# Image-wise adapter stack on one core: the second product with x2 as the stationary operand and W2 streamed in 512 columns

## The chip, the cores and the metric

The kernel runs on one core of a Trainium2 chip. The metric is device time in microseconds (us) of one execution. Before the change the median of three runs is 509.82 us (509.17 to 510.21).

The core's engines work side by side and meet at semaphores only: PE (TensorE, matmuls into the PSUM banks; its weight loads have a row of their own, PEld), DVE (VectorE), ACT (ScalarE), POOL (GpSimd), and SP (SyncE), which here issues every DMA.

## The reference

The inputs are 8 images x of 256 rows (tokens) by 1024, all float32. For each image, with `a` and `l` the two adapter numbers of that image:

```python
x0 = x + dequantise(x)                      # 8 thresholds, 8 deltas, 8 zero points
x1 = x0                                     # called x1 in the kernel
x2 = x1 + x1 @ W1[a].T                      # W1: 8 matrices 1024x1024
x3 = x2 + x2 @ W2.T + 0.5*(x2 @ A2[l]) @ B2.T     # W2 1024x1024, rank 32
out = x3 + (x3 @ B3[a].T) @ A3[a].T         # rank 16
```

`dequantise` takes for each element the group that its absolute value falls in, rounds x/delta, clips it to 64 levels and multiplies back; above the largest threshold it gives 0.

## The kernel before

**Layout.** The 1024 features are 8 tiles (k or o) of 128 partitions; the 256 tokens lie along the free dimension. An image is 8 x 256 columns on 128 partitions, worked in two chunks of 4 tiles (1024 columns).

**Quantiser.** Per image 16 steps, 8 groups for each chunk. ACT makes `tq` and `mask`, DVE makes the level (`value`, L499), clips it (`clamp`, L509) and lays it over `y` by the mask (`select`, L523). At a chunk's end `cut_y` (L529) and `add_y` (L534) write that chunk of x1. The quantiser runs one image ahead of the matmuls, so DVE and ACT carry the small jobs of image b in fixed slots between the steps of image b+1. The slots are tables of step numbers (`ACT_X2`, `DVE_X2`, `W2_AT` and others), one column for the first images and one for the later.

**W1 phase.** PE multiplies in full float32 (`w1b` stationary, x1 of 256 columns moving, L742) into four banks `x2_bank`, one for each pair of output tiles: first all output tiles with the first chunk of x1, then with the second. A float32 matmul leaves two records in the trace, so that the 64 matmuls of an image are 128 records.

**x2.** As a pair is done, DVE adds x1 (`finish_x2`, L588) into a tile x2, ACT rounds that to float32r (`x2h`, L381), and DVE takes the remainder (`x2l`, L595).

**Second product.** The identity was added to W2 once, and W2 was split into `w2h` and `w2l`, and so into three products per tile: w2h with x2h, w2l with x2h, w2h with x2l. Each is a float32r matmul with a 128x128 tile of W2 stationary and x2 of 256 columns moving (L709, 192 for an image). The low-rank part goes through `low_bank` (L715, 24 matmuls with `vh`, `vl`), is rounded into `lows`, and comes back with `uhh` and `ul0` (L726, L727: 2 matmuls for each of the 8 output tiles, 16 for an image). The tables behind v and u (A2 with G = B3 + B3 W2, and E = B2 + A3 (B3 B2) with A3) are chosen per image by DMA from DRAM and rounded and split again on ACT and DVE for each image (`round_v`, `split_v` L603, `round_u`, `split_u` L608).

**Start.** PE first makes the 8 tiles of G and the four blocks of E. W2 comes in slices of 512 KB into two places `stage`; for each slice POOL adds the identity (L317), ACT rounds (L407), POOL takes the remainder (L319).

**Order of the work.** Each engine executes its list in program order; SP's one queue likewise, so that a DMA stands behind every wait that SP passes before it.

Of the kernel before, what the change touches and what calls it, by code (L numbers as in the profile page):

```python
# [5 lines left out]
def quantised_residual_adapter_stack(nc, x, params, w1, w2t, w2n, b3t, b2n, b2r, a3, la, ids_b, ids_a,  # L6
                                     own_rows, low_scale, ident, out, e_dram, g_dram):

# [22 lines left out]
    ALU = mybir.AluOpType  # L31
# [7 lines left out]
    NL = la.shape[0]  # L39
# [9 lines left out]
    OUT_BANKS = 2  # L49
# [5 lines left out]
    TQ, MK = 4, 2  # L55

    ctx = ExitStack()
    with ctx:
# [12 lines left out]

        xin = sb("xin", [P, KT, T])
        x1 = sb("x1", [P, KT, T])
        x2 = sb("x2", [P, 2, 2 * T])
        x2h = sb("x2h", [P, KT, T], f32r)
        x2l = sb("x2l", [P, KT, T], f32r)
        outb = sb("outb", [P, PAIRS, 2 * T])
        w1b = sb("w1b", [P, OT, KT * P])
        w2h = sb("w2h", [P, OT, KT * P], f32r)
        w2l = sb("w2l", [P, OT, KT * P], f32r)  # L80
        stage = sb("stage", [P, 2, KT * P])
# [12 lines left out]
        scrap = sb("scrap", [P, 2])  # L94
        lscale = sb("lscale", [P, 1])
        ua = sb("ua", [P, D])
        uhh = sb("uhh", [P, D], f32r)
        ul0 = sb("ul0", [P, D], f32r)
        va = sb("va", [P, KT, R2])
        vg = sb("vg", [P, KT, R3])  # L100
        vh = sb("vh", [P, KT, P], f32r)
        vl = sb("vl", [P, KT, P], f32r)
        lowh = sb("lowh", [P, T], f32r)
        lows = sb("lows", [P, T], f32r)
        ycut = uq[:, 1, :]

        b3s = chunk(x1, 1).rearrange("p (k r) -> p k r", k=KT)
        a3s = outb[:, 0:2, :].rearrange("p j t -> p (j t)")
        b2s = outb[:, 2, 0:KT * R2].rearrange("p (k r) -> p k r", k=KT)
        dmask = outb[:, 2, KT * R2:KT * R2 + NA * R2].rearrange("p (a r) -> p a r", a=NA)  # L110
        eye = outb[:, 3, 0:P]
        rows = outb[:, 3, P:P + NA]
        gsb = ua[:, :].rearrange("p (a k r) -> p a k r", a=NA, k=KT)
        b2rep = x2[:, :, :].rearrange("p j t -> p (j t)")
        w2g = w1b
        e_place = [outb[:, 0, :], outb[:, 1, :], outb[:, 2, :], x2[:, 1, :]]


        x2_bank = [pb(f"x2_bank{i}") for i in range(PAIRS)]
        out_bank = [pb(f"out_bank{i}") for i in range(OUT_BANKS)]  # L120
        low_bank = pb("low_bank")
        de_bank = pb("de_bank")
        e_bank = [low_bank, de_bank] + out_bank

# [4 lines left out]
        b_in = sem("b_in")  # L129
        small_in = sem("small_in")  # L130
        w2g_in = [sem(f"w2g_in{j}") for j in range(KT // 2)]
        stage_in = [sem(f"stage_in{c}") for c in range(2)]
        u_in = sem("u_in")
        v_in = sem("v_in")

        store_done = [sem(f"store_done{c}") for c in range(2)]
        pads = sem("pads")
        ua_zero = sem("ua_zero")
# [9 lines left out]
        x1_ready = sem("x1_ready")  # L148
        pair_done = sem("pair_done")
        x2_ready = sem("x2_ready")  # L150
        out_ready = sem("out_ready")
        e_out = sem("e_out")
        diag_ready = sem("diag_ready")
        x2h_ready = sem("x2h_ready")
        x2l_ready = sem("x2l_ready")
        vh_ready = sem("vh_ready")
        vl_ready = sem("vl_ready")
        uh_ready = sem("uh_ready")
        ul_ready = sem("ul_ready")
# [4 lines left out]
        dmask_ready = sem("dmask_ready")  # L164
        g_tiles = sem("g_tiles")
        g_ready = sem("g_ready")
        e_done = sem("e_done")
        e_ready = sem("e_ready")
# [5 lines left out]
        def group_of(s):  # L174

            return G - 1 - s % G
# [5 lines left out]
        def x2_pairs(n):  # L182

            return PAIRS + n

        def out_pairs(n):

            return OUT_BANKS + n


        @block.sync
        def _(sp):
# [10 lines left out]
            def load_u(a):  # L203
                for r in (0, DUP):
                    sp.dma_start(ua[r:r + R2, :], e_dram[bass.ds(a, 1)].rearrange("a r n -> (a r) n")) \
                        .then_inc(u_in, 16)
                    sp.dma_start(ua[r + R2:r + R, :], a3[bass.ds(a * R3, R3), :]).then_inc(u_in, 16)

            def load_v(a, lab):
                sp.dma_start(va[:, :, :], la[bass.ds(lab, 1)].rearrange("a p k r -> (a p) k r")) \  # L210
                    .then_inc(v_in, 16)
                sp.dma_start(vg[:, :, :], g_dram[bass.ds(a, 1)].rearrange("a p k r -> (a p) k r")) \
                    .then_inc(v_in, 16)
# [24 lines left out]
            a0, lab0 = ids_of(0)  # L238


            def store_e(e, done):
                h, n = divmod(e, 2)
                sp.wait_ge(e_ready, e + 1)
                sp.dma_start(e_dram.rearrange("(h a) r n -> h (a r) n", h=EH)[h, :, n * 512:(n + 1) * 512],
                             e_place[e]).then_inc(done, 16)

            def load_w2(i):

                sp.dma_start(stage[:, i % 2, :], w2t[i, :, :]).then_inc(stage_in[i % 2], 16)

            load_w2(0)
            load_w2(1)
# [3 lines left out]
            sp.wait_ge(g_ready, 2)  # L256
            sp.dma_start(g_dram.rearrange("a p k r -> p a k r"), gsb[:, :, :, :]).then_inc(store_done[0], 16)
            sp.wait_ge(x1_ready, 1)
            load_x(1, 0)
            sp.wait_ge(store_done[0], 16)  # L260
            load_v(a0, lab0)
            E_AFTER = (3, 3, 4, 4)
            for i in range(2, OT):
                if i == OT // 2:
                    sp.wait_ge(x1_ready, 2)
                    load_x(1, 1)
                sp.wait_ge(w2l_ready, i - 1)
                load_w2(i)
                for e in range(2 * EH):
                    if i == E_AFTER[e]:  # L270
                        store_e(e, e_out if e < 2 * EH - 1 else store_done[1])
                if i == E_AFTER[-1] + 1:
                    sp.wait_ge(store_done[1], 16)
                    sp.wait_ge(e_out, 16 * (2 * EH - 1))
                    sp.wait_ge(ua_zero, 1)
                    load_u(a0)

            def next_batch(b, ahead):

                a, lab = ids_of(b + 1)  # L280
                for j in range(PAIRS):
                    sp.wait_ge(pair_done, 2 * PAIRS * b + j + 1)
# [4 lines left out]
                sp.wait_ge(vl_ready, 4 * (b + 1))  # L287
                sp.wait_ge(ul_ready, b + 1)
                load_v(a, lab)
                load_u(a)  # L290
                for c in range(2):
                    sp.wait_ge(out_ready, out_pairs(PAIRS * b + 2 * c + 2))
                    store(b, c)
                if ahead:
                    sp.wait_ge(x1_ready, 2 * (b + 1) + 2)
                    load_x(b + 2, 1)

# [3 lines left out]
            for j in range(PAIRS):  # L301
                sp.wait_ge(out_ready, out_pairs(PAIRS * LAST + j + 1))
                sp.dma_start(out[LAST, :, j, :], outb[:, j, :]).then_inc(store_done[j // 2], 16)
            for c in range(2):
                sp.wait_ge(store_done[c], 16 * (B + 2))
# [3 lines left out]
        def _(pool):  # L309
# [4 lines left out]
            for o in range(OT):  # L314
                pool.wait_ge(stage_in[o % 2], 16 * (o // 2 + 1))
                diag = stage[:, o % 2, o * P:(o + 1) * P]
                nc.gpsimd.tensor_tensor(diag, diag, eye, ALU.add).then_inc(diag_ready, 1)  # L317
                pool.wait_ge(w2h_ready, o + 1)
                nc.gpsimd.tensor_tensor(w2l[:, o, :], stage[:, o % 2, :], w2h[:, o, :].bitcast(f32),  # L319
                                        ALU.subtract).then_inc(w2l_ready, 1)  # L320
                if o == 1:
                    pool.wait_ge(store_done[0], 16)
                    nc.gpsimd.memset(ua[:, :], 0.0).then_inc(ua_zero, 1)

        D_AT, G_AT = 9, (10, 12)
        E_AT = (STEPS + 2, STEPS + 2, STEPS + 3, STEPS + 3)
        W2_AT = (11, 14, 16, 17, STEPS + 5, STEPS + 6, STEPS + 7, STEPS + 9)  # L330
# [3 lines left out]
        ACT_V, DVE_V = 2, 3  # L334
        ACT_U, DVE_U = (7, 4, 4, 4), (8, 5, 5, 5)
        ACT_X2 = ((4, 5, 6, 7), (6, 7, 8, 9), (7, 8, 9, 10), (8, 9, 10, 10))
# [7 lines left out]
        def _(act):  # L344
# [47 lines left out]
            def round_u(b, first):  # L392
                act.wait_ge(u_in, 64 * (b + 1))
                if not first:
                    act.wait_ge(pair_done, 2 * PAIRS * b)
# [443 lines left out]
```

## Time and profile before

| what | before |
|---|---|
| median of 3 runs | 509.82 us |
| span of the profiled execution | 508.2 us (the records hold no other time of that execution) |
| PE busy | 479.8 us, 94% |
| DVE busy | 437.5 us, 86% |
| ACT busy | 356.1 us, 70% |
| POOL busy | 36.8 us, 7% |
| DMA | 67.0 MB, 132 GB/s over the span |
| granted clock of PE, mean | 0.979 of full |

The span runs from the first to the last instruction of the profiled execution, 1.6 us less than the median of the runs. A busy share is the time in which the engine had at least one instruction under way. Matmuls overlap in the pipeline (a record of 0.28 us starts every 0.12 us), so the cost of one is read from the distance of the starts, never from its own length.

### The profile page before, as it was taken

The page shows a single profiled execution, that of the slowest core. Times are in us where ns is not written, and L with a number is a line of the kernel's source. Part 1 is how long each engine was busy: PE and PEld are TensorE (multiplying, and loading weights), DVE is VectorE, ACT ScalarE, POOL GpSimd, SP SyncE. Part 2 cuts the span into 40 slices and gives each one's busy share as a digit, 9 for nine tenths or more (in the row PEclk, how much of TensorE's full clock was granted, in tenths as well). Part 3 has the DMA queues.
Part 4 walks back from the last instruction along what each step waited for, and adds up shares of the span by engine and source line. Part 5 has one row for each costly group of instructions (what it writes and reads, how often), then busy time and mean ns, then how long its engine had stood idle before and what let it go on. Part 6 is the DMA issues. An engine that isn't in the chain of part 4 may idle for free.

```text
span 508.2 us, 8219 instructions
## 1 busy us (share of the span) xinstructions
PE 479.8 (94%) x3056; PEld 446.1 (88%) x3056; DVE 437.5 (86%) x521; ACT 356.1 (70%) x400; POOL 36.8 (7%) x24
## 2 busy tenths in 40 slices
PE   3979589799999999999999999999999999999997
PEld 3968278798899989998899989998899889998997
DVE  4999999999999999999999989998999979941300
ACT  6996767798878796798778866987498867710110
POOL 2123407600000000000000000000000000000000
PEclk9979879899999999999999999999999999999999
DMA  8965161660284027410661057402741246110011
GB/s 283 414 271 182 42 195 53 268 226 2 83 331 130 0 67 278 157 41 36 221 235 50 0 164 251 126 0 83 258 160 41 78 170 212 41 41 0 0 41 41
DMA packets 18112, 67.00 MB, mean 132 GB/s; under 512 B 2608, under 2 KB 5936, under 8 KB 14000
## 3 DMA queue, kind: packets, MB, share of 16 engines
q1 hardware_dynamic: 18096, 66.81, 37.8%
q8 instruction: 7, 0.11, 0.1%
q14 instruction: 9, 0.07, 0.0%
HBM read 56.84 MB, written 9.96 MB: 131 GB/s over the span
## 4 chain that ended last, share of the span: by engine, by line
PE 58%; DVE 28%; issue 6%; POOL 3%; ACT 2%; DMA 1%; DVEq 0%; SPq 0%; ACTq 0%
PE x_bank L742 28%; PE out_bank L709 25%; DVE y L523 11%; DVE uq L509 6%; DVE tq L499 4%; PE low_bank L715 3%; POOL w2l L319 2%; DVE uq L529 2%; DVE x L534 2%; DVE x2l L595 1%; DVE y L509 1%; PE out_bank L727 1%; PE out_bank L726 1%; ACT tq L352 1%; DMA xin<-x 1%
## 5 line engine op out<-in xcount | busy, mean ns | idle before, releaser
L742 PE MATMUL x_bank<-x,w1b 128*128 128x256 f32 x1024 | 227.8, 385 | 11.5 <-DVE x L534 11.5
L742 PEld LDWEIGHTS x_bank<-x,w1b 128*128 128x128 f32 x1024 | 197.6, 194 | 40.0 <-DVE x L534 12.6
L352 ACT ACTIVATE tq<-xin,magic,rdelta 128x1024 f32<-128x1024 f32 x128 | 157.4, 1232 | 3.5 <-DMA xin<-x 3.2
L368 ACT ACTIVATE mask<-absx,negtop 128x1024 bf16<-128x1024 f32 x112 | 128.2, 1144 | 36.4 <-DVE y L523 34.5
L523 DVE COPY_PREDICATED y<-mask,uq 128x1024 f32<-128x1024 int16 x112 | 150.5, 1344 | 0.1
L709 PE MATMUL out_bank<-x2h,w2h 128*128 128x256 f32 x512 | 145.5, 284 | 0.4 <-ACT outb L414 0.4
L709 PE MATMUL out_bank<-x2h,w2l 128*128 128x256 f32 x512 | 145.4, 284 | 0.0
L709 PE MATMUL out_bank<-x2l,w2h 128*128 128x256 f32 x512 | 145.2, 284 | 0.0
L499 DVE TENSOR_SCALAR tq<-tq,par 128x1024 f32<-128x1024 f32 x128 | 109.6, 856 | 5.8 <-ACT tq L352 3.9
L709 PEld LDWEIGHTS out_bank<-x2h,w2h 128*128 128x128 f32 x512 | 98.5, 192 | 0.6 <-ACT outb L414 0.6
L709 PEld LDWEIGHTS out_bank<-x2h,w2l 128*128 128x128 f32 x512 | 98.7, 193 | 0.0
L709 PEld LDWEIGHTS out_bank<-x2l,w2h 128*128 128x128 f32 x512 | 98.7, 193 | 0.0
L509 DVE TENSOR_SCALAR uq<-tq,ylow,yhigh 128x1024 f32<-128x1024 f32 x112 | 93.4, 834 | 1.1 <-issue 0.9
L381 ACT ACTIVATE x2h<-x 128x512 fp32r<-128x512 f32 x32 | 20.0, 625 | 54.0 <-DVE x L588 53.9
L588 DVE TENSOR_TENSOR x<-x_bank,x 128x512 f32<-128x512 f32 x32 | 21.9, 685 | 27.1 <-PE x_bank L742 27.0
L414 ACT ACTIVATE outb<-out_bank 128x512 f32<-128x512 f32 x32 | 18.6, 582 | 19.2 <-PE out_bank L727 19.2
L361 ACT ACTIVATE absx<-xin 128x1024 f32<-128x1024 f32 x16 | 16.9, 1054 | 19.1 <-DVE uq L529 19.1
L319 POOL TENSOR_TENSOR w2l<-stage,w2h 128x1024 fp32r<-128x1024 f32 x8 | 25.6, 3198 | 29.3 <-ACT w2h L407 29.3
L595 DVE TENSOR_TENSOR x2l<-x,x2h 128x512 fp32r<-128x512 f32 x32 | 22.0, 689 | 3.2 <-ACT x2h L381 2.8
L529 DVE SCALAR_TENSOR_TENSOR uq<-absx,top,y 128x1024 f32<-128x1024 f32 x16 | 20.6, 1285 | 0.4
L715 PE MATMUL low_bank<-x2h,vh 128*128 128x256 f32 x64 | 19.6, 307 | 1.3 <-DVE x2l L595 1.3
L726 PE MATMUL out_bank<-lows,uhh 128*128 128x256 f32 x64 | 17.0, 287 | 3.4 <-DVE lows L613 3.4
(64 smaller groups left out, 284.7 us busy)
## 6 DMA issues: line engine op xcount, KB each, us to landing
w1b<-w SPq DMA_DIRECT2D x32, 1024.0 KB, 4.9
xin<-x SPq DMA_DIRECT2D x16, 512.0 KB, 4.7
out<-outb SPq DMA_DIRECT2D x14, 512.0 KB, 2.8
w1b<-w2n SPq DMA_DIRECT2D x4, 1024.0 KB, 12.0
stage<-w2t SPq DMA_DIRECT2D x8, 512.0 KB, 5.3
ua<-e_dram SPq DMA_DIRECT2D x16, 128.0 KB, 3.6
va<-la SPq DMA_DIRECT2D x8, 128.0 KB, 3.7
ua<-a SPq DMA_DIRECT2D x16, 64.0 KB, 3.6
```

What stands on the lines that cost most here:

```text
L319: nc.gpsimd.tensor_tensor(w2l[:, o, :], stage[:, o % 2, :], w2h[:, o, :].bitcast(f32), ALU.subtract).then_inc(w2l_ready, 1)
L352: nc.scalar.activation(tq[:, s % TQ, :], chunk(xin, c), ACT.Identity, bias=magic[:, 0:1], scale=rdelta[:, g:g + 1]).then_inc(t_ready, 1)
L368: nc.scalar.activation(mask[:, s % MK, :], absx[:, :], ACT.Relu, bias=negtop[:, g:g + 1], scale=1.0).then_inc(mask_ready, 1)
L499: nc.vector.tensor_scalar(tq[:, s % TQ, :], tq[:, s % TQ, :], -MAGIC, par[:, 1, g:g + 1], ALU.add, ALU.mult).then_inc(u_ready, 1)
L509: nc.vector.tensor_scalar(clamped_y, tq[:, s % TQ, :], ylow[:, g:g + 1], yhigh[:, g:g + 1], ALU.max, ALU.min).then_inc(clamped, 1)
L523: nc.vector.copy_predicated(y[:, :], mask[:, s % MK, :].bitcast(i16), uq[:, s % 2, :]) \
L529: nc.vector.scalar_tensor_tensor(ycut, absx[:, :], top[:, G - 1:G], y[:, :], ALU.is_gt, ALU.mult).then_inc(y_cut, 1)
L595: nc.vector.tensor_tensor(x2l[:, pair, :].rearrange("p k t -> p (k t)"), x2[:, j % 2, :], x2h[:, pair, :].rearrange("p k t -> p (k t)").bi ...
L709: nc.tensor.matmul(into, w[:, o, cut], xs[:, k, :], start=(o % 2 == 0 and k == 0 and i == 0), stop=False, skip_group_check=True)
L715: last = nc.tensor.matmul(low_bank[:, 0:T], v[:, k, :], xs[:, k, :], start=(k == 0 and i == 0), stop=(k == KT - 1 and i == 2), skip_group_ ...
L726: nc.tensor.matmul(into, uhh[:, cut], lows[:, :], start=False, stop=False, skip_group_check=True)
L742: last = nc.tensor.matmul(x2_bank[j][:, (o % 2) * T:(o % 2 + 1) * T], w1b[:, o, k * P:(k + 1) * P], x1[:, k, :], start=(o % 2 == 0 and k = ...
```

## The change

The diff touches nearly every part; the rows of x2 and W2 swap their roles, and work moves between engines.

- **Second product.** 128 tokens of x2 are the stationary operand and 512 output columns of W2 (now held by input tile k) stream past it. An image is 4 accumulators `acc` (2 token tiles by 2 halves of the output) x 8 tiles k x 3 = 96 matmuls of 512 columns instead of 192 of 256; u_low has 8 of 512 instead of 16 of 256. The output leaves token-major.
- **x1 in x2.** POOL adds the identity to the 8 diagonal tiles of W1 of each image (`w1_diagonals`), and `finish_x2` goes; ACT rounds from PSUM straight into x2h, DVE subtracts from PSUM. PE waits for `w1_ready`.
- **Low-rank tables.** A2, A3, G and E are each split into a rounded part and a remainder once, at the start, and all kept in DRAM. Per image 8 DMAs for v and 6 for u bring the ready halves straight into `vh`, `vl`, `uhh`, `ul0` (before: 2 and 4). ACT's and DVE's splits per image go. `vh` and `vl` are stored with k innermost, so that a stationary tile `v[:, :, k]` takes every eighth element.
- **Start.** The remainder of W2 moves from POOL to DVE (`DVE_W2`). The E blocks come before the first W1 phase, behind a wait for the split of G. `low_bank` shares a bank with `x2_bank[0]`.
- **Waits.** PE waits for three pairs of x2l before V, where it waited for two.

```diff
-        vh = sb("vh", [P, KT, P], f32r)
+        vh = sb("vh", [P, P, KT], f32r)
+        low_bank = x2_bank[0]
...
+            for k in range(ST):
+                w2_diagonal(k)
+            w1_diagonals(0)
+            for k in range(ST, KT):
+                w2_diagonal(k)
+            with pool.Fori(1, B) as b:
+                w1_diagonals(b)
...
             def split_x2(b, j):
                 dve.wait_ge(x2h_ready, PAIRS * b + j + 1)
                 pair = slice(2 * j, 2 * j + 2)
-                nc.vector.tensor_tensor(x2l[:, pair, :].rearrange("p k t -> p (k t)"), x2[:, j % 2, :],
+                nc.vector.tensor_tensor(x2l[:, pair, :].rearrange("p k t -> p (k t)"), x2_bank[j][:, :],
...
             def v_x2(tiles):
+
                 for k in tiles:
                     for i, (v, xs) in enumerate(((vh, x2h), (vl, x2h), (vh, x2l))):
-                        last = nc.tensor.matmul(low_bank[:, 0:T], v[:, k, :], xs[:, k, :],
+                        last = nc.tensor.matmul(low_bank[:, 0:T], v[:, :, k], xs[:, k, :],
...
+            def product(q, k):
+                t, h = divmod(q, 2)
+                cols = slice(h * DH, (h + 1) * DH)
+                for i, (xs, w) in enumerate(((x2h, w2h), (x2h, w2l), (x2l, w2h))):
+                    nc.tensor.matmul(acc[q][:, :], xs[:, k, t * P:(t + 1) * P], w[:, k, cols],
+                                     start=(k == 0 and i == 0), stop=False, skip_group_check=True)
...
+                for e in range(2 * EH):
+                    h, n = divmod(e, 2)
+                    half = slice(n * DH, (n + 1) * DH)
+                    if e == 2:
+                        pe.wait_ge(gh_ready, 2)
+                        pe.wait_ge(gl_ready, 2)
...
+        ACT_LA, DVE_LA = 3, 4
+        ACT_A3, DVE_A3, DVE_D = 4, 5, 5
+        ACT_G, DVE_G = 10, 11
+        ACT_E, DVE_E = (12, 12, 13, 13), (13, 13, 14, 14)
+        ACT_W2, DVE_W2 = (9, 10, 12, 13, 15, 16, 18, 19), (10, 11, 13, 14, 16, 17, 19, 20)
```

Three places show what moves. First DVE between the first and the second chunk of x1 of image 0, behind the `add_y` of the first chunk. Before:

```order
L534 TENSOR_TENSOR x<-xin,uq 128x1024
L499 TENSOR_SCALAR tq<-tq,par 128x1024
L509 TENSOR_SCALAR uq<-tq,ylow,yhigh 128x1024
L499 TENSOR_SCALAR tq<-tq,par 128x1024
L509 TENSOR_SCALAR uq<-tq,ylow,yhigh 128x1024
L523 COPY_PREDICATED y<-mask,uq 128x1024
```

And now (L590 is the remainder of a W2 slice, L580 that of G, L585 that of E):

```order
L506 TENSOR_TENSOR x<-xin,uq 128x1024
L590 TENSOR_TENSOR w2l<-stage,w2h 128x1024
L475 TENSOR_SCALAR tq<-tq,par 128x1024
L484 TENSOR_SCALAR uq<-tq,ylow,yhigh 128x1024
L580 TENSOR_TENSOR x<-acc,uhh 128x128x4
L580 TENSOR_TENSOR x<-acc,uhh 128x128x4
L590 TENSOR_TENSOR w2l<-stage,w2h 128x1024
L475 TENSOR_SCALAR tq<-tq,par 128x1024
L484 TENSOR_SCALAR uq<-tq,ylow,yhigh 128x1024
L496 COPY_PREDICATED y<-mask,uq 128x1024
```

Three operations on 1024 or 512 columns have come in ahead of two quantiser steps; more of them (E and W2) follow before the second chunk. Second, PE from the end of G's tiles to the first W1 phase. Before:

```order
L698 MATMUL out_bank<-x,w1b 128x128 x8
L742 MATMUL x_bank<-x,w1b 128x256 x32
L687 MATMUL low_bank<-x,outb 128x512
L688 MATMUL low_bank<-outb 128x512
L687 MATMUL de_bank<-x,outb 128x512
```

And now (with what each waits for):

```order
L664 MATMUL acc<-x,w1b 128x128 x8
L679 MATMUL acc<-outb,eye 128x512 [waits dmask_ready,small_in]
L680 MATMUL acc<-outb,dmask 128x512
L679 MATMUL acc<-outb,eye 128x512
L680 MATMUL acc<-outb,dmask 128x512
L679 MATMUL acc<-outb,eye 128x512 [waits gl_ready,gh_ready]
L680 MATMUL acc<-outb,dmask 128x512
L679 MATMUL acc<-outb,eye 128x512
L680 MATMUL acc<-outb,dmask 128x512
L690 MATMUL x_bank<-x,w1b 128x256 [waits w1_ready,x1_ready]
```

E stands ahead of the first W1 phase, and a wait for DVE's split of G with it. Third, DVE where it meets the pairs of x2 (a step of the quantiser with one pair). Before:

```order
L588 TENSOR_TENSOR x<-x_bank,x 128x512 [waits x2l_ready,pair_done]
L499 TENSOR_SCALAR tq<-tq,par 128x1024 [waits t_ready]
L509 TENSOR_SCALAR uq<-tq,ylow,yhigh 128x1024 [waits y_ready,u_ready,mask_ready,clamped]
L595 TENSOR_TENSOR x2l<-x,x2h 128x512 [waits x2h_ready]
L523 COPY_PREDICATED y<-mask,uq 128x1024
```

And now:

```order
L475 TENSOR_SCALAR tq<-tq,par 128x1024 [waits t_ready]
L484 TENSOR_SCALAR uq<-tq,ylow,yhigh 128x1024 [waits y_ready,u_ready,mask_ready,clamped]
L552 TENSOR_TENSOR x2l<-x_bank,x2h 128x512 [waits x2h_ready]
L496 COPY_PREDICATED y<-mask,uq 128x1024
```

The add at the head of the step is gone; DVE meets the pair after its own two operations, and through ACT only.

## Rows read from the trace of the kernel before

**Rows 1.** The page: busy time, share of the span, instructions.

```profile
PE 479.8 (94%) x3056; PEld 446.1 (88%) x3056; DVE 437.5 (86%) x521; ACT 356.1 (70%) x400; POOL 36.8 (7%) x24
```

**Rows 2.** The chain in order of time, image 4: start us, us, what.

```profile
283.60 27.63 PE x_bank L742 x128
...
332.73 5.75 PE out_bank L709 x48
...
338.95 27.63 PE x_bank L742 x128
```

**Rows 3.** PE's timeline: start us, us, line, what; G's tiles, then a half-clock stretch.

```profile
17.93 0.39 PE L696 MATMUL out_bank<-x,outb 128*128 128x128 f32 x2
...
19.94 0.39 PE L696 MATMUL out_bank<-x,outb 128*128 128x128 f32 x2
...
97.95 0.41 PE L709 MATMUL out_bank<-x2h,w2h 128*128 128x256 f32 x1
...
100.51 0.41 PE L709 MATMUL out_bank<-x2h,w2h 128*128 128x256 f32 x1
```

**Rows 4.** Windows: busy us by engine, then PE's clock, DMA share, GB/s.

```profile
97.90:100.60 2.70, 2.70 (x15) 2.70 (x14) 2.69 (x2) 1.73 (x2) 0.90 (x1) 0.50 1.00 422
```

**Rows 5.** PE's timeline: starts of the phases of images 0 to 2.

```profile
33.65 16.94 PE L742 MATMUL x_bank<-x,w1b 128*128 128x256 f32 x64 [3.50 <-DVE x L534]
...
65.49 16.38 PE L742 MATMUL x_bank<-x,w1b 128*128 128x256 f32 x64 [8.04 <-DVE x L534]
...
81.53 0.47 PE L715 MATMUL low_bank<-x2h,vh 128*128 128x256 f32 x1
...
115.05 27.79 PE L742 MATMUL x_bank<-x,w1b 128*128 128x256 f32 x128
...
172.01 27.79 PE L742 MATMUL x_bank<-x,w1b 128*128 128x256 f32 x128
```

**Rows 6.** Groups by line, DVE, 33.5 to 65.4 us (POOL at work).

```profile
L499 DVE TENSOR_SCALAR tq<-tq,par 128x1024 f32<-128x1024 f32 x9 | 13.5, 1504 | 0.2 <-DVE y L523 0.2
...
L509 DVE TENSOR_SCALAR uq<-tq,ylow,yhigh 128x1024 f32<-128x1024 f32 x7 | 8.0, 1137 | 0.0
```

**Rows 7.** Groups by line, DVE, 103.8 to 126.4 us (POOL idle).

```profile
L523 DVE COPY_PREDICATED y<-mask,uq 128x1024 f32<-128x1024 int16 x7 | 9.4, 1340 | 0.0
...
L499 DVE TENSOR_SCALAR tq<-tq,par 128x1024 f32<-128x1024 f32 x8 | 5.9, 739 | 0.2 <-DVE y L523 0.2
...
L509 DVE TENSOR_SCALAR uq<-tq,ylow,yhigh 128x1024 f32<-128x1024 f32 x7 | 5.6, 803 | 0.0
```

**Rows 8.** POOL's timeline: one remainder of W2, one identity add.

```profile
44.68 2.58 POOL L319 TENSOR_TENSOR w2l<-stage,w2h 128x1024 fp32r<-128x1024 f32 x1 [5.96 <-ACT w2h L407]
...
72.17 0.45 POOL L317 TENSOR_TENSOR stage<-stage,outb 128x128 f32<-128x128 f32 x1 [11.79 <-DMA stage<-w2t]
```

**Rows 9.** Groups by form, whole span: xcount, busy us, mean ns, idle before.

```profile
L595 DVE TENSOR_TENSOR x2l<-x,x2h 128x512 fp32r<-128x512 f32 x32 | 22.0, 689 | 3.2 <-ACT x2h L381 2.8
...
L381 ACT ACTIVATE x2h<-x 128x512 fp32r<-128x512 f32 x32 | 20.0, 625 | 54.0 <-DVE x L588 53.9
...
L603 DVE TENSOR_TENSOR vl<-va,vh 128x256 fp32r<-128x256 f32 x16 | 6.7, 419 | 0.0
...
L608 DVE TENSOR_TENSOR ul<-ua,uhh 64x1024 fp32r<-64x1024 f32 x8 | 9.7, 1208 | 1.1 <-ACT uhh L396 1.1
```

**Rows 10.** DVE's timeline: beside an identity add, and at pair 0 of image 4.

```profile
72.16 1.01 DVE L499 TENSOR_SCALAR tq<-tq,par 128x1024 f32<-128x1024 f32 x1
...
300.91 0.69 DVE L588 TENSOR_TENSOR x<-x_bank,x 128x512 f32<-128x512 f32 x1 [1.63 <-PE x_bank L742]
```

**Rows 11.** Windows again, 20 to 25 us; the last number is GB/s.

```profile
20.00:25.00 5.00, 5.00 (x47) 5.00 (x47) 5.00 (x7) 4.89 (x5) 1.13 (x1) 1.00 1.04 417
```

**Rows 12.** The page's DMA issues: KB each, us to landing.

```profile
stage<-w2t SPq DMA_DIRECT2D x8, 512.0 KB, 5.3
```

**Rows 13.** ACT's timeline: the copy of the last bank.

```profile
505.05 0.60 ACT L414 ACTIVATE outb<-out_bank 128x512 f32<-128x512 f32 x1 [5.57 <-PE out_bank L727]
```

More of the change, by code:

```diff
@@ L488, in _ @@
             batch(LAST, 0)
-            finish_out(LAST, PAIRS - 2)
-            finish_out(LAST, PAIRS - 1)
+            for q in range(ACCS):
+                finish_out(LAST, q)
         @block.vector
@@ L702, in product, with bilinear @@
-            def product(o, tiles):
-                into = out_bank[o // 2 % OUT_BANKS][:, (o % 2) * T:(o % 2 + 1) * T]
-                for k in tiles:
-                    cut = slice(k * P, (k + 1) * P)
-                    for i, (w, xs) in enumerate(((w2h, x2h), (w2l, x2h), (w2h, x2l))):
-                        nc.tensor.matmul(into, w[:, o, cut], xs[:, k, :], start=(o % 2 == 0 and k == 0 and i == 0),
-                                         stop=False, skip_group_check=True)
+            def bilinear():
+                pe.wait_ge(b_in, 64)
+                for k in range(KT):
+                    last = nc.tensor.matmul(de_bank[:, 0:R2], b3s[:, k, :], b2s[:, k, :],
+                                            start=(k == 0), stop=(k == KT - 1))
+                last.then_inc(d_done, 1)
@@ new lines, in adapters_g @@
+            def adapters_g():
+                for i in range(KT):
+                    if i % 2 == 0:
+                        pe.wait_ge(w2g_in[i // 2], 16)
+                    into = g_bank[i // HALF][:, (i % HALF) * P:(i % HALF + 1) * P]
+                    nc.tensor.matmul(into, eye[:, :], b3s[:, i, :], start=True, stop=False)
+                    for o in range(OT):
+                        last = nc.tensor.matmul(into, w2g[:, i, o * P:(o + 1) * P], b3s[:, o, :],
+                                                start=False, stop=(o == OT - 1))
+                    last.then_inc(g_tiles, 1)
@@ new lines, in adapters_e @@
+            def adapters_e():
+                per = P // R2
+                pe.wait_ge(small_in, 48)
+                pe.wait_ge(dmask_ready, 1)
+                for e in range(2 * EH):
+                    h, n = divmod(e, 2)
[3 more added lines that the diff above has]
+                        pe.wait_ge(gl_ready, 2)
+                    nc.tensor.matmul(e_bank[e][:, :], eye[:, :], b2rep[:, half], start=True, stop=False)
+                    nc.tensor.matmul(e_bank[e][:, :], dmask[:, h * per:(h + 1) * per, :].rearrange("p a r -> p (a r)"),
+                                     a3s[:, half], start=False, stop=True).then_inc(e_done, 1)
@@ new lines, in w1_x1 @@
+            def w1_x1(b, c):
+                pe.wait_ge(x1_ready, 2 * b + c + 1)
+                for o in range(OT):
+                    j = o // 2
+                    if c == 0 and o % 2 == 0:
+                        pe.wait_ge(w1_ready, OT * b + 2 * (j + 1))
+                    for k in range(c * HALF, (c + 1) * HALF):
+                        last = nc.tensor.matmul(x2_bank[j][:, (o % 2) * T:(o % 2 + 1) * T],
+                                                w1b[:, o, k * P:(k + 1) * P], x1[:, k, :],
+                                                start=(o % 2 == 0 and k == 0), stop=(k == KT - 1),
+                                                skip_group_check=True)
+                    if c == 1 and o % 2 == 1:
+                        last.then_inc(pair_done, 1)
```

568 lines of the change are left out of this document (277 added, 291 removed).

## The prediction

> **What bounds the kernel now.** I read the page's busy shares first: PE 94%, DVE 86% [rows 1]. Two engines near the top need the chain in order of time to tell which one sets the end. In image 4 the chain is PE alone: W1 takes 27.63 us, and from one W1 phase to the next it is 338.95 - 283.60 = 55.35 us, without a gap [rows 2]. So the later images are bound by PE, and the second part of an image (V, the products, U: 24 + 192 + 16 = 232 matmuls) takes 55.35 - 27.63 = 27.72 us, 0.1195 us each; a stretch of 48 gives 5.75/48 = 0.1198 [rows 2]. W1 costs 27.63/128 = 0.2159 us a record [rows 2].
>
> The early images are another matter. PE stood 8.04 us before the second half of W1 of image 0, waiting for DVE's x1 at 65.49 [rows 5]. From there image 0 needs 13.8 + 27.7 = 41.5 us at full clock, but image 1 starts at 115.05, 49.6 us later [rows 5]: 8.1 us are lost to waits and to half clock (the half W1 phase alone lasted 81.53 - 65.49 = 16.0 instead of 13.8). Images 1 and 2 lose another 1.6 and 0.9 us: 115.05 to 172.01, and to 228.25, which is 283.60 less a period [rows 2, 5]. From image 3 on nothing is lost. So the end is: the time of x1's second chunk of image 0, plus image 0, plus seven periods of PE, plus the tail of 508.2 - 505.05 = 3.15 us [rows 13].
>
> **The products.** 96 matmuls of 512 columns take the place of 192 of 256, and in U 8 that of 16. The trace has no float32r matmul of 512 columns, so I bound it. Below: a float32 record of 256 columns streams two passes, 512 column times, in 0.2159 us [rows 2], so 512 columns cannot go faster than about 0.216. Above: twice 0.1197, 0.239, no gain. Which one depends on what sets 0.1197 at 256 columns, which is 0.012 above half of 0.2159. At half clock (granted clock 0.50, [rows 4]) the same matmuls follow each other in (100.51 - 97.95)/12 = 0.2133 us [rows 3], just 256 columns at 1.2 GHz, with no excess. And float32 records of 128 columns (two passes) take 2.01/18 = 0.1117 [rows 3], also above half. So the excess shows where the stream lasts about as long as the weight load and goes where the stream is longer. I take 0.216; 104 of them are 22.5 us. With V at 24 x 0.1195 = 2.9 an image is 27.63 + 2.9 + 22.5 = 52.95 us, **2.4 less**.
>
> **V.** The same 24 matmuls, but the stationary tile takes every eighth element. No row shows a strided weight load. Below: nothing. Above: a second weight slot per matmul, another 0.1195 us, since the load is what these matmuls wait for. I take nothing, as an engine that reads one element per partition and step has no reason in the rows to mind the step; this is my weakest term. The Trainium skill (Advanced Engine Details and Errata, SBUF Cachelines) says that SBUF lines are 16 bytes and that taking a different line at each access costs; a step of 8 floats is 32 bytes. By that rule the sum would go to the upper bound, 23 us more. No row here shows it.
>
> **DVE in the later images.** It loses `finish_x2`, 4 x 0.69 [rows 10], the four splits of v (0.42 the larger ones, some 1.4 together) and 1.2 for u [rows 9]: 5.3 us. It gets POOL's eight identity adds in its way. Beside the one such add that stood alone (0.45 us on POOL, [rows 8]) DVE's `value` took 1.01 instead of 0.74 us [rows 7, 10]: 0.27 x 8 = 2.2. It waited 1.63 us for pair 0 in image 4 [rows 10], so its slack becomes 1.6 + 5.3 - 2.2 - 2.4 = 2.3 us: PE stays the bound. ACT (70%) loses work too.
>
> PE now waits for x2l of three pairs at the end T of W1. Pair 2 is done 3.45 us before T (an eighth of 27.63); then ACT 0.63 and DVE 0.69 [rows 9]. DVE is not free at once: after pair 0 (T - 10.4, split by T - 9.0) it has select 1.3, value and clamp 1.5, split 0.7, select 1.3, value 0.7 [rows 7], then the split of pair 2, which ends near T - 2 with ACT's part. No gap, 2 us of cushion. `low_bank` shares a bank with pair 0 and `lows` of the image before is long done. The 14 DMAs per image (8 and 6, some 1.4 MB, 3.3 us of the queue at 417 GB/s, [rows 11]) lie under a 53 us period; v is called for 25 us before use and u more. `w1_ready` comes 20 us early.
>
> **The start.** x1's second chunk came at 65.49. What goes: POOL's remainders of W2, 2.58 us each [rows 8], hold DVE up. Between the chunks DVE's `value` took 1.504 us on average and `clamp` 1.137 [rows 6], with POOL idle 0.739 and 0.803 [rows 7]: 9 x 0.765 + 7 x 0.334 = 9.2 us. What comes before that point, with 1.2 us for 1024 columns and 0.69 for 512 [rows 9]: six W2 remainders 7.2, A3 1.2, A2 (1280 columns) 1.5, G 1.4, E 2.8, the mask 0.4 (256 columns): 14.5. So 65.5 - 9.2 + 14.5 = 70.8. Then waits. W2's slice 2 is asked for only behind the wait for G's split (step 11) on SP; it lands 5.3 us later [rows 12], POOL 0.45 [rows 8] and ACT 1.3 (1024 columns, twice 0.63) follow, 7.0 in all, while DVE has two steps of some 2.6 (value, clamp and select, less their overlap, [rows 7]) and half of E, 6.6. But the queue also carries 3.0 MB more by then (A2 in, its halves and A3's out), 7 us at 417 GB/s [rows 11], and slice 5 stands behind two 1 MB stores of E. I estimate 4 us of waits (bounds 0 and 10): **x1 at 74.8**, 9.3 later than before.
>
> The first half of W1 of image 0 (16.9 us, [rows 5]) now starts behind G's split. The first chunk comes at 33.65 [rows 5] plus A2, A3 and the mask, 3.1; then a W2 remainder, value and clamp, and G, 4.1: 41. Behind that stand two blocks of E, eight records of twice W1's columns, 3.5 us. From 44.5 the half phase ends at 61, or at 72 if all of it ran at half clock (64 x 0.432), still before 74.8: hidden. If it were not, each us of it would count.
>
> Image 0 after that: the half phase 16.0 as before, since PE has idled again [rows 5], 1 us for pair 2 (W2's slice 7 waits for x1 on SP and holds ACT), V, products and U 25.4. POOL's 9 us per image of remainders and the wait for W2 are over by then. Image 1 starts at 74.8 + 42.4 = 117.2, 2.2 later than before. DVE then reaches x1 of image 1, second chunk, near 129, and PE wants it at 131.
>
> **Sum.** 117.2 + 7 x 52.95 = 487.9, + 3.15 = 491.0 us of span, against 508.2. Check by differences: + 2.2 (start), - 7 x 2.4 = - 16.8, - 2.5 (gaps of images 1 and 2): - 17.1. The median of the runs lies 1.6 us above the profiled span: 492.7; with a little for the cushions, **493 us**.
>
> **Rivals.**
> *V's strided load takes a second slot* (the other side). PE's rows in V would stand 0.239 us apart; 192 matmuls x 0.1195 = 23 us, all on PE's path: 516 us, slower. It decides from (509.8 - 493)/192 = 0.088 us per matmul. For it speaks that 0.1197 already looks bound by the load; against it nothing in the rows. 0.25.
> *512 columns cost twice 256.* 104 x 0.023 x 8 = 19 us more: 512 us. The half-clock rows and the 128-column rows speak against it. 0.06.
> *The start runs later*, waits of 14 us instead of 4, by the queue: 503 us. 0.10.
> *DVE becomes the bound*: an identity add stops it for longer than 0.27 us (0.9 us each would be 7.2 instead of 2.2, 5 us against a slack of 2.3, so 2.7 x 7 = 19 us, 512 at the worst), or pair 2 comes 2 us late each image. Half of that, 503 us. 0.08.
> *As forecast*: 0.49, from 486 (no waits for W2: -4, and 3 us in which the first half phase of image 0 runs warm) to 503 (waits of 10, and an excess of 0.01 us left per matmul of 512, 8 us, not both in full). Nothing of these: 0.02.
>
> **Range and chances.** A change below 0.2%, 1 us, cannot be told from none. Faster: 0.49 + 0.10 + 0.08 + 0.02 and a part of the load's case (a penalty below 0.088 us), 0.71 in all; same 0.04; slower 0.25. The likeliest case's own range is 486 to 503. The range over all must reach into the strided load's case: 486 to 516.
>
> **What the profile would show.** Right: product records 0.216 us apart and 96 an image; V's 0.12 apart; W1 phases 53 us apart from image 1 or 2 on; DVE's x1 of image 0 near 75 with waits at the W2 remainders; DVE's `value` near 0.75 us in the start. Wrong: V at 0.2 or more; a period set by DVE, with PE idle before V or before W1; x1 beyond 80. The prediction falls mostly by V's load, then by the start.

## The result and the profile after

The changed kernel takes **525.53 us** (median of 4 runs, 524.54 to 525.86) against 509.84 for the kernel before, measured beside it: a ratio of 1.0307, 95% interval [1.0292, 1.0321]. It is 3% slower. The forecast was 493, a gain, with a range of 486 to 516: the change went the other way, and the time lies 9.5 us above the range. The profiled execution's span is 523.9 us (508.2 before).

The page's busy row answers to [rows 1]:

```profile
PE 489.1 (93%) x2224; PEld 422.9 (81%) x2224; DVE 408.9 (78%) x464; ACT 336.7 (64%) x354; POOL 72.3 (14%) x79
```

PE has 832 instructions fewer (3056 before), VectorE 57, ScalarE 46, and VectorE is 28.6 us less busy. PE, with all these instructions gone, is 9.3 us *more* busy. So some of its instructions became dearer. The chain in order of time (start us, us, what) shows which, in image 4; it answers to [rows 2]:

```profile
292.98 27.63 PE x_bank L690 x128
320.60 4.26 PE x_bank L701 x18
324.86 5.48 PE acc L711 x24
330.35 1.33 PE x_bank L701 x6
331.68 8.20 PE acc L711 x36
...
349.92 10.14 PE x_bank L690 x47
```

The chain is PE alone, as before, without a gap. L690 is W1 and costs what it did. L701 is V: (4.26 + 1.33)/24 = 0.233 us a matmul, where 0.1195 was reckoned. L711 is the 512-column product: 5.48/24 = 0.2283, 8.20/36 = 0.2278, where 0.216 was reckoned. The period is 349.92 - 292.98 = **56.95** us; before it was 55.35, the forecast 52.95.

The weight loads of the same matmuls, as groups by line over the whole span (xcount, busy us, mean ns, idle before):

```profile
L711 PEld LDWEIGHTS acc<-w2h,x2h 128*128 128x128 f32 x256 | 48.6, 190 | 9.8
...
L701 PEld LDWEIGHTS x_bank<-x2h,vl 128*128 128x128 f32 x64 | 21.6, 338 | 0.0
```

Both load 128x128 elements of one type. The one takes neighbouring elements and 190 ns, the other every eighth element and 338 ns. The last column of V's loads is 0.0: one load follows the other. That the matmuls wait for them is so far a reading; the first experiments test it.

In the start, PE's timeline (start us, us, line, what, idle before and its releaser) answers to [rows 5]:

```profile
48.44 13.98 PE L690 MATMUL x_bank<-x,w1b 128*128 128x256 f32 x64
...
74.21 15.48 PE L690 MATMUL x_bank<-x,w1b 128*128 128x256 f32 x64 [11.79 <-DVE x L506]
...
91.87 0.49 PE L701 MATMUL x_bank<-x2h,vh 128*128 128x256 f32 x1 [2.18 <-DVE x2l L552]
```

x1's second chunk of image 0 comes at 74.2 (forecast 74.8, before 65.5). PE then waits 2.18 us for the low parts of x2. Image 1 starts at 122.13; the chain has it as

```profile
122.13 3.02 PE x_bank L690 x14
```

The difference of the two spans, added up: image 1 starts 122.13 - 115.05 = 7.1 us later; seven periods of 1.6 us more give 11.2; the gaps of images 1 and 2 before [rows 2, 5] are gone, 2.5 less. Together 15.8, and 523.9 - 508.2 = 15.7.

### The profile page after: what moved, and what is told of

It reads as the page before. It is cut to its first block, busy times and chain, and to the rows that moved or that the text cites. A ratio compares the mean times of both kernels' runs of the same rounds, so it can differ in the third digit from the quotient of the medians.

```text
span 523.9 us, 6604 instructions
## 1 busy us (share of the span) xinstructions
PE 489.1 (93%) x2224; PEld 422.9 (81%) x2224; DVE 408.9 (78%) x464; ACT 336.7 (64%) x354; POOL 72.3 (14%) x79
## 4 chain that ended last, share of the span: by engine, by line
PE 82%; SPq 6%; DMA 4%; DVE 3%; issue 3%; ACT 2%; POOL 0%; DVEq 0%; POOLq 0%; ACTq 0%
PE x_bank L690 37%; PE acc L711 34%; PE x_bank L701 9%; DMA stage<-w2t 2%; DMA a3l_dram<-x 2%; PE acc L720 1%; PE acc L718 1%; SPq L244 1%; SPq L211 1%; DVE y L496 1%; SPq L210 1%; ACT tq L361 1%; ACT mask L376 1%; SPq L206 1%; SPq L219 1%
## 5 line engine op out<-in xcount | busy, mean ns | idle before, releaser
L690 PE MATMUL x_bank<-x,w1b 128*128 128x256 f32 x1024 | 224.0, 381 | 11.8 <-DVE x L506 11.8
L690 PEld LDWEIGHTS x_bank<-x,w1b 128*128 128x128 f32 x1024 | 195.4, 191 | 39.7 <-DVE x L506 12.2
L329 POOL TENSOR_TENSOR w1b<-w1b,eye 128x128 f32<-128x128 f32 x64 | 63.7, 1015 | 315.8 <-DMA w1b<-w 315.8
L711 PE MATMUL acc<-w2h,x2l 128*128 128x512 f32 x256 | 100.2, 391 | 0.0
L711 PE MATMUL acc<-w2l,x2h 128*128 128x512 f32 x256 | 100.1, 391 | 0.0
L711 PE MATMUL acc<-w2h,x2h 128*128 128x512 f32 x256 | 100.0, 391 | 0.0
L711 PEld LDWEIGHTS acc<-w2h,x2h 128*128 128x128 f32 x256 | 48.6, 190 | 9.8
L711 PEld LDWEIGHTS acc<-w2h,x2l 128*128 128x128 f32 x256 | 48.2, 188 | 10.3
L711 PEld LDWEIGHTS acc<-w2l,x2h 128*128 128x128 f32 x256 | 48.2, 188 | 9.9
L701 PE MATMUL x_bank<-x2h,vh 128*128 128x256 f32 x64 | 25.8, 404 | 2.2 <-DVE x2l L552 2.2
L701 PE MATMUL x_bank<-x2l,vh 128*128 128x256 f32 x64 | 26.1, 407 | 0.0
L701 PE MATMUL x_bank<-x2h,vl 128*128 128x256 f32 x64 | 26.0, 407 | 0.0
```

The costliest lines, as they stand in the source:

```text
L329: nc.gpsimd.tensor_tensor(diag, diag, eye[:, :], ALU.add).then_inc(w1_ready, 1)
L690: last = nc.tensor.matmul(x2_bank[j][:, (o % 2) * T:(o % 2 + 1) * T], w1b[:, o, k * P:(k + 1) * P], x1[:, k, :], start=(o % 2 == 0 and k = ...
L701: last = nc.tensor.matmul(low_bank[:, 0:T], v[:, :, k], xs[:, k, :], start=(k == 0 and i == 0), stop=(k == KT - 1 and i == 2), skip_group_ ...
L711: nc.tensor.matmul(acc[q][:, :], xs[:, k, t * P:(t + 1) * P], w[:, k, cols], start=(k == 0 and i == 0), stop=False, skip_group_check=True)
```

## The experiments

Theory A: V's weight load with a step of 32 bytes costs a second slot, about 0.12 us a matmul, and this alone turns the gain into a loss. Theory B: the start and its waits, or VectorE beside GpSimd's additions, did it. A smaller question is why 512 columns cost 0.228 and not 0.216 us.

### V's step alone: every, every second, every fourth element

The three kernels differ from the changed one in this alone (s is 1, 2 or 4; the tables in SBUF keep their order, so V is multiplied with its elements in the wrong places):

```diff
-    last = nc.tensor.matmul(low_bank[:, 0:T], v[:, :, k], xs[:, k, :],
+    view = v.rearrange("p r k -> p (r k)").rearrange("p (c s) -> p c s", s=s)
+    last = nc.tensor.matmul(low_bank[:, 0:T], view[:, (k // s) * P:(k // s + 1) * P, k % s], xs[:, k, :],
```

> The changed kernel, with one thing altered: the stationary tiles of V are read as 128 neighbouring elements from the same two buffers instead of every eighth element, so that the low-rank part is computed with scrambled tables (the output is not the reference's); counts, loads and waits are the same. Theory 1, the step slows the weight load: V's records stand 0.12 us apart instead of 0.237, an image takes 56.95 - 24 x 0.118 = 54.1 us, and the whole 525.5 - 8 x 2.8 = 503 us. Rival, V is slow because its sums go to the bank that pair 0 used, or because of what DMA writes: V stays near 0.237 us and the time near 525.5.

> As the run with neighbouring elements, but every second element (8 bytes from one to the next), tables scrambled again. If each new 16-byte line costs only when it is hit less than twice (the Trainium skill, Advanced Engine Details and Errata, SBUF Cachelines), two of every line are taken and V stays at 0.12 us a record, about 503 us; if any step but one costs, 0.237 and 525.

> As before with every fourth element (16 bytes from one to the next). If the penalty is for taking a new 16-byte line at each access, V is at 0.237 us as with every eighth, about 525 us; if it grows with the distance, V lies between 0.12 and 0.237.

Measured: 501.58 us (501.13 to 501.90; ratio to before 0.9841 [0.9825, 0.9858]) with neighbouring elements, 502.63 with every second, 523.99 with every fourth (one run each for these two). The chain's rows of V in image 4, for steps of 1, 2 and 4 elements, one fence for each kernel:

```profile
307.47 2.06 PE x_bank L702 x18
```

```profile
308.33 2.15 PE x_bank L702 x18
```

```profile
319.70 4.10 PE x_bank L702 x18
```

That is 0.114, 0.119 and 0.228 us a matmul, and 4.26/18 = 0.237 for the changed kernel's step of 8. The weight loads of V show the same, for steps of 1 and 4 elements:

```profile
L702 PEld LDWEIGHTS x_bank<-x2h,vl 128*128 128x128 f32 x64 | 12.1, 189 | 0.5
```

```profile
L702 PEld LDWEIGHTS x_bank<-x2h,vl 128*128 128x128 f32 x64 | 20.9, 327 | 0.0
```

The price hardly grows with the step. It jumps between 8 bytes, where two columns share 16 bytes, and 16 bytes, where each column has its own; no step between the two was tried. The Trainium skill (Advanced Engine Details and Errata, SBUF Cachelines) has lines of 16 bytes, and at least two hits on one are needed to hide the access. The trace agrees. In medians the step is worth 525.53 - 501.58 = **23.95 us**, where theory A's 192 x 0.12 is 23.0. About 1 us of it isn't the step's: x1 of image 0, ahead of all of V, came at 73.18 us there and at 74.21 in the changed kernel, and with the full step it came at 73.19 in another run (the one with 256 columns below).

### The step in the kernel before

The same edit the other way round: the kernel before, with V's stationary tile taken as every eighth element of its table (again the elements are in the wrong places).

```diff
-    last = nc.tensor.matmul(low_bank[:, 0:T], v[:, k, :], xs[:, k, :],
+    view = v.rearrange("p k r -> p (k r)").rearrange("p (c s) -> p c s", s=KT)
+    last = nc.tensor.matmul(low_bank[:, 0:T], view[:, :, k], xs[:, k, :],
```

> The kernel before, with the stationary tiles of V taken as every eighth element of the same buffers (tables scrambled, so the output is not the reference's), nothing else altered. Theory 1: V goes from 0.1195 to 0.237 us a record, 24 x 0.118 x 8 = 22.6 us, 532 us. Rival (V's pace in the changed kernel is not the step's doing): 510 us, as before.

Measured: 526.92 us (526.49 to 527.30), ratio 1.0338 [1.0320, 1.0355]: 17 us more, not 22.6. Two rows of the chain, W1 of images 4 and 5:

```profile
289.12 27.63 PE x_bank L743 x128
...
347.30 27.63 PE x_bank L743 x128
```

The period is 58.18, longer than 55.35 by 2.83 = 24 x 0.118, as expected. But image 4 starts only 289.12 - 283.60 = 5.5 us later and not 11.3: the first images of the kernel before are not bound by PE [rows 5], and part of a slower PE disappears in their waits. The expected sum had charged all eight images in full. V has a bank of its own in this kernel, so the bank that V shares in the changed one isn't the cause.

### The width of the products

Three kernels change the columns of a product matmul: two of 256 in place of one of 512 (the whole computation), only 384 of the 512 columns, and only 128 of them (the others of each product are left out).

```diff
-    nc.tensor.matmul(acc[q][:, :], xs[...], w[:, k, cols], ...)
+    for c0 in range(0, WIDTH, N):
+        nc.tensor.matmul(acc[q][:, c0:c0 + N], xs[...], w[:, k, h * DH + c0:h * DH + c0 + N], ...)
```

> The changed kernel with the second product in 256 columns again (192 matmuls an image, x2 still stationary, V still strided). Theory, a float32r matmul costs its columns at 2.4 GHz plus a fixed 0.012 to 0.015 us: 0.1197 us a record as in the kernel before, an image 56.95 + 192 x 0.1197 - 96 x 0.2283 = 58.0 us, 8.5 us more in all, 534 us. Rival, x2 as the stationary operand sets its own pace: another spacing than 0.1197 at 256 columns.

> The changed kernel with only 384 of each 512 columns of the second product (a quarter of the product is left out). Fixed cost per matmul: 384/2.4 = 0.160 plus 0.013 to 0.015, 0.174 us a record. Cost in proportion to the columns, from the 512-column rows: 0.171; from the 256-column rows: 0.180.

> The changed kernel with only 128 of each 512 columns (three quarters of the product left out). If the weight load is what 256-column matmuls wait for, the records stay near 0.12 us apart; if the excess is a fixed cost per matmul on top of the stream, 0.053 + 0.013 = 0.067 us.

Measured: 534.66 us (ratio to before 1.0494 [1.0477, 1.0512]), 486.83 and 474.49 (one run each for these two). Rows of the chain, one fence each for 256, 384 and 128 columns:

```profile
328.36 5.75 PE acc L712 x48
```

```profile
306.42 4.17 PE acc L712 x24
```

```profile
351.69 3.97 PE acc L712 x36
```

A matmul costs 0.1198 us at 256 columns, 0.1738 at 384, 0.2283 at 512. Columns at 2.4 GHz would be 0.1067, 0.1600 and 0.2133; the rest is 0.0131, 0.0138 and 0.0150. So a matmul of the product pays 13 to 15 ns on top of its stream at full clock, at all three lengths. At 256 columns this is what the kernel before had with W2 stationary (0.1198, [rows 2]), so the swapped roles don't change it. It isn't a constant of every float32r matmul: V's 18 with neighbouring elements, 256 columns too, stand 2.06/18 = 0.1144 apart, 8 ns above the stream. At 128 columns a matmul costs 3.97/36 = 0.1103 with the granted clock at 1.00, far above the stream (0.0533). There the weight load is the likely floor: the 768 loads of the product have 1.4 us of idle time between them all, against 30.0 at 512 columns. Merging two 256-column matmuls into one saves one such 14 ns, not the excess of both: 534.66 - 525.53 = **9.1 us** for the kernel, where 19 were forecast (2.4 x 8, with U's matmuls in it).

### V as every second element, the whole computation

`vh` and `vl` become four groups of 128 columns by 2, so that the step is 8 bytes; the DMA's runs are then 256 and 128 bytes instead of whole rows.

```diff
-        vh = sb("vh", [P, P, KT], f32r)
+        vh = sb("vh", [P, KT // 2, P, 2], f32r)
...
-    sp.dma_start(tile[:, r:r + R2, :]..., la_from[...].rearrange("a p n -> (a p) n"))
+    sp.dma_start(tile[:, :, r:r + R2, :]..., la_from[...].rearrange("a p (b n) -> (a p) b n", n=R2 * 2))
...
-    last = nc.tensor.matmul(low_bank[:, 0:T], v[:, :, k], xs[:, k, :],
+    last = nc.tensor.matmul(low_bank[:, 0:T], v[:, k // 2, :, k % 2], xs[:, k, :],
```

> The changed kernel, complete, with vh and vl laid out as pairs of k innermost (a stationary tile takes every second element) and DMA runs of 256 and 128 bytes instead of 1024 and 512. Theory 1: V at 0.12 us a record and 502 to 503 us, as in the run with every second element. Rival: the four times as many DMA pieces slow the loads of W1, x and v, PE waits for v or W1, and the time stays above 510 us.

Measured: **502.82 us** (501.73 to 503.74), ratio 0.9862 [0.9842, 0.9882]: 1.4% faster than the kernel before and 4.3% faster than the changed one. Image 4 in the chain:

```profile
281.44 27.63 PE x_bank L692 x128
309.07 2.15 PE x_bank L703 x18
311.22 5.47 PE acc L713 x24
316.69 0.72 PE x_bank L703 x6
317.40 8.20 PE acc L713 x36
...
335.65 27.63 PE x_bank L692 x128
```

V costs 0.1194 again and the period is 54.21.

### V as neighbouring elements, the whole computation

As the last kernel with groups of one, so that the DMA's runs are 128 and 64 bytes.

> The whole computation, with V's stationary columns neighbouring elements in SBUF (step of 4 bytes) in place of every second element (8 bytes): the DMA's runs are 128 and 64 bytes instead of 256 and 128. If the load depends only on whether at least two columns share 16 bytes, V's products stay at 0.115-0.12 us and the time at 502-504 us; if the DMA's smaller pieces land late, V of image 0 waits longer than 1.7 us and the time is 504-510 us.

Measured: 505.15 us (one run). The load does what was expected, 2.06 us for 18 and a period of 54.09. But image 1 starts 2.6 us later than with groups of two. Two stretches of the chain tell why, the first with groups of two, the second with groups of one:

```profile
69.84 4.23 DMA stage<-w2t
...
92.02 1.09 PE x_bank L703 x7
```

```profile
61.59 2.80 SPq L206
...
72.27 3.46 DMA stage<-w2t
```

SP issues the 14 DMAs of V and U ahead of W2's slice 6. The eight issues of V take 5.6 us from first to last with whole rows, 7.3 with groups of two and 9.5 with groups of one, where the longest (L206, pieces of 128 bytes) holds SP for 2.80 us; the slice goes out at 72.27 instead of 69.84 (67.69 in the changed kernel with whole rows). ScalarE waits for it in its fixed order, the low parts of x2 behind it come later, and PE's timeline has

```profile
93.24 0.55 PE L703 MATMUL x_bank<-x2h,vh 128*128 128x256 f32 x1 [2.45 <-DVE x2l L554]
```

With groups of two this wait is 1.73 us, and V starts 1.2 us earlier. The other 1.4 of the 2.6 us are half clock behind the wait: from V's first matmul to the product's it is 93.24 to 96.91, 3.67 us, and 2.25 with groups of two. So small pieces cost here by what they delay on the queue. What makes the issues long isn't shown: from 61.50 to 64.40 us the DMA engines are busy all the time (share 1.00) and move 248 GB/s, where with whole rows they move 340 (61.50 to 64.30, share 0.98), so slower transfers that hold up the queue aren't ruled out.

### Where the start is bound

A third place for the staged float32 weights, so that W2's third slice needs no wait (part of the staging of A2 moves to another buffer, and slice 7 is asked for ahead of the next x):

```diff
-    TQ, MK, ST = 4, 2, 2
+    TQ, MK, ST = 4, 2, 3
```

> The whole computation, as in fix2, with three places instead of two for the staged float32 weights, so that the third W2 slice is loaded before anything has to free a place. In the kernel after, the wait for that slice was the last link of the chain in the start (5.6 us), and PE waited 1.7 to 2.2 us for x2's low parts before V of image 0. If the start is bound by the chain of loads, W1 of image 0's second half moves from 74.1 to 68-70 us and the time from 502.8 to 496-499 us. If it is bound by DVE's sum of work (the rival), the time stays at 502-503 us: the same work is done in the same order, only earlier waited for. All images after the first should keep the period of fix2, about 54.1 us.

Measured: 502.36 us (501.68 to 503.21), ratio to before 0.9856 [0.9840, 0.9873], against [0.9842, 0.9882] for the kernel with two places. No difference that the runs can tell; the rival holds. PE's timeline:

```profile
74.26 15.99 PE L697 MATMUL x_bank<-x,w1b 128*128 128x256 f32 x64 [8.89 <-DVE x L511]
```

VectorE's windows show why, here of the kernel with two places (length, then busy us of PE, PEld, DVE, ACT, POOL, then clock, DMA share, GB/s):

```profile
33.00:74.00 41.00, 21.41 (x77) 14.96 (x75) 39.28 (x45) 25.58 (x29) 10.28 (x12) 0.80 0.84 270
```

VectorE is busy for 39.28 of the 41 us up to x1; with three places it is 39.34 of 41.3. A chain that goes through a load is no proof that the load binds: with the load early, VectorE's sum of work ended at the same time.

### W2's remainder back on GpSimd

```diff
+                pool.wait_ge(w2h_ready, k + 1)
+                nc.gpsimd.tensor_tensor(w2l[:, k, :], stage[:, k % ST, :], w2h[:, k, :].bitcast(f32), ...)
-                    if s == DVE_W2[k]:
-                        dve.wait_ge(w2h_ready, k + 1)
-                        nc.vector.tensor_tensor(w2l[:, k, :], ...)
```

> The whole computation, as in fix2, with W2's remainders back on GpSimd. Prediction's theory: GpSimd's subtractions beside DVE slow both (DVE's lines of the start took 1504 and 1137 ns in the kernel before), so moving them to VectorE was worth about what it cost DVE; then the second half of image 0's W1 starts within 3 us of 74.1 and the time is 501-506 us. Rival: W2's remainder on VectorE is what holds the start up, and returning it to GpSimd frees about 9 us of DVE: time 495-498 us. From image 1 on nothing should change.

Measured: 508.51 us (506.55 to 510.15), ratio 0.9983 [0.9966, 1.0000]. The remainder on VectorE is worth 5.7 us, so both expectations missed: x1 came more than 3 us later, and the time is above 506. Groups by line in 33 to 75 us, VectorE and GpSimd:

```profile
L502 DVE COPY_PREDICATED y<-mask,uq 128x1024 f32<-128x1024 int16 x8 | 12.8, 1601 | 0.0
L481 DVE TENSOR_SCALAR tq<-tq,par 128x1024 f32<-128x1024 f32 x9 | 11.2, 1244 | 5.8 <-ACT tq L367 3.8 <-DMA a3l_dram<-x 1.8 <-DVE y L502 0.2
...
L340 POOL TENSOR_TENSOR w2l<-stage,w2h 128x1024 fp32r<-128x1024 f32 x7 | 19.3, 2764 | 6.3 <-ACT w2h L434 6.3
```

and with the remainder on VectorE:

```profile
L498 DVE COPY_PREDICATED y<-mask,uq 128x1024 f32<-128x1024 int16 x8 | 10.5, 1309 | 0.0
L477 DVE TENSOR_SCALAR tq<-tq,par 128x1024 f32<-128x1024 f32 x10 | 7.9, 786 | 2.7 <-DMA a3l_dram<-x 2.1 <-ACT mask L378 0.6
```

`value` takes 1244 ns beside GpSimd's subtractions and 786 without. The longest, 2.85 us from 63.28, stands beside a subtraction of 2.35 us from 63.23. In addition VectorE waits 3.8 us for ScalarE, which stands in its order behind W2's slices. x1 comes at 78.7 instead of 74.1. Up to there VectorE is busy for 41.1 of 45.7 us (39.3 of 41 with the remainder on it), 1.8 more, though its six remainders (7.5 us) are gone. So the slower operations cost some 9.3 us and the longer waits 2.9.

### GpSimd's additions

The additions of the identity to W1 are left out:

```diff
-                    for o in (2 * j, 2 * j + 1):
-                        diag = w1b[:, o, o * P:(o + 1) * P]
-                        nc.gpsimd.tensor_tensor(diag, diag, eye[:, :], ALU.add).then_inc(w1_ready, 1)
```

> fix2 without the additions of the identity to W1's tables on GpSimd: the value of x1 is missing in the sum of each block, so this part of the computation is left out. It prices these additions. If they only slow VectorE's evictions (value 775 ns), those fall to about 740 ns and the time stays within 0.5 us of 502.8, since PE is the bound. If W1's products wait for them somewhere, PE's period falls below 54 us and the time by over 1 us.

Measured: 501.75 us (one run). The four runs with the additions spread from 501.73 to 503.74, so this time alone decides nothing between the two cases. VectorE's busy time falls from 408.9 to 401.9, and its `value` over the whole span from 779 to

```profile
L472 DVE TENSOR_SCALAR tq<-tq,par 128x1024 f32<-128x1024 f32 x128 | 96.9, 757 | 8.3 <-ACT tq L358 4.0 <-DMA a3l_dram<-x 2.1 <-DVE y L493 1.3
```

The period stays 54.21, so PE doesn't wait for the additions. They slow VectorE by 7.0/8 = 0.9 us an image, which from image 1 on costs no time. Image 1 starts 1.5 us earlier (117.36 for 118.82), 0.9 of it at x1 (73.25 for 74.13); x1 differs by as much between runs that have the additions, so what they cost in image 0 isn't shown.

## Why the prediction was wrong, by its own steps

**The step that failed: V.** "The same 24 matmuls, but the stationary tile takes every eighth element [...] I take nothing." Its upper bound, a second slot of 0.1195 us, was the truth: 0.118 us a matmul in the kernel before, some 23 us for the changed kernel. The ground given was that no row speaks for a cost; but no row spoke against it either, and the case for a cost, which the Trainium skill's rule on 16-byte lines (Advanced Engine Details and Errata, SBUF Cachelines) supports, was put into a rival at 0.25. That rival had 516 us. That its price came out so near is partly luck: it took the slot of 0.1195 for the load's own, but the floor at 128 columns is 0.110.

**A term of the wrong size: 512 columns.** Forecast 0.216, measured 0.228: 104 x 0.012 x 8 = 10 us. The inference "the excess shows where the stream lasts about as long as the weight load and goes where the stream is longer" is refuted by 384 and 512 columns, where the stream is well above that floor of 0.110 and 14 and 15 ns remain. The rows at half clock [rows 3, 4], on which it leant, were read as if what vanishes there vanished for every long stream. This is why the time went beyond the rival's 516.

**From 491.0 to 523.9 in spans.** The period is 4.0 us longer than forecast (V 5.59 for 2.9; products and U 23.73 for 22.5), seven times: 28. Image 1 starts at 122.13 instead of 117.2: V 2.7, columns 1.3, the wait for the third pair 2.18 instead of 1, and the rest half clock behind this wait, less 0.6 at x1 and 0.5 in W1: 4.9. Sum 32.9. The tail, 3.1 us, is as before.

**What held.** PE is the bound of the later images, without a gap. x1's second chunk came at 74.21 for 74.8, in part by luck, as the 4 us of waits within it were mostly in another place: 2.26 us stood ahead of the first chunk,

```profile
33.50 0.75 DVE L475 TENSOR_SCALAR tq<-tq,par 128x1024 f32<-128x1024 f32 x1 [2.26 <-DMA a3l_dram<-x]
```

and 0.24, 0.34 and 0.58 between the chunks, 3.4 in all. W2's slices cost VectorE next to no wait, and the gain of [rows 6] over [rows 7] came true: `value` took 787 ns in the start. The first half of W1 of image 0 began at 48.44, not 44.5, and is still hidden. The additions cost 0.9 us an image, not 2.2. The loads of V and U are hidden from image 1 on; in image 0 they hold SP ahead of a slice of W2, which was not foreseen.

**Theory B** falls: without V's step the same start gives 501.58 us, faster than the kernel before. What is left against 493 is 8.6 us: the period is 54.09 for 52.95, 8.0 us in seven, and image 1 starts at 117.58 for 117.2.

**Open:** why the product's matmuls pay 13 to 15 ns and V's with neighbouring elements 8, while a float32 record of 256 columns pays only 2.6 above twice its stream (0.2159 against 0.2133, [rows 2]), and why nothing of it is left at half clock [rows 3]. No kernel took these apart. What brings PE back to half clock behind a pause wasn't tried either.

## What to carry to other kernels

Before a layout is changed to save copies, look at the step of the stationary operand in bytes. At steps of 16 and 32 bytes a matmul of 256 columns took twice what it takes at 4 and 8 here; groups of two float32 elements brought the kernel from 525.5 to 502.8 us and still save the copies. Where a cost is in no row, the better estimate is the bound for which something speaks, not zero; and a small excess per instruction should be measured at a second size before it is argued away. A wait in the chain is worth removing only if the engine behind it isn't busy anyway.

## What the hardware showed unexpectedly

The cost of a step in the weight load is a jump: 0.114 and 0.119 us a matmul at 4 and 8 bytes, 0.228 and 0.237 at 16 and 32. The loads themselves take 189, 196, 327 and 338 ns. At half clock the changed kernel's V matmuls are hardly slower: from 94.44 to 96.13 us they stand 0.241 apart. So what sets the pace of such a load doesn't halve with the granted clock.

A short pause of PE was followed by half clock in some runs. Behind the changed kernel's 2.18 us wait the windows' clock (last but two) falls to 0.50 some 3 us later, in the kernel with V in groups of one behind 2.45 us to 0.53; in the kernel with groups of two, behind 1.73 us, it stays 1.00. With W2's remainder on GpSimd the wait was 2.85 us and the clock 1.00 in the 6 us around it, so the length of the pause alone doesn't decide. It costs 1.0 us in the changed kernel (V's 18 and the product's 24 matmuls take 10.72 us in the chain, 9.74 in image 4) and 1.4 with groups of one. The changed kernel's window:

```profile
95.00:97.00 2.00, 2.00 (x9) 0.50 0.00 0
```

A DMA with short runs occupied the queue that issues it for longer. Of the eight issues of V's tables in image 0, six took 0.34 to 0.38 us with whole rows, six 0.54 to 0.67 with runs of 256 and 128 bytes, and five 0.57 to 0.73 with 128 and 64. The longest took 1.54, 1.77 and 2.80.
